# TensorE's products beside the sort handed out whole, six matmuls in a row, instead of in two parts of three

## What is computed

```
gate_feature = hidden_states * pe[i] @ gate_w + gate_b
gate_weight, gate_idx = jax.lax.top_k(gate_feature, K)          # K = 384 of 768
gate_weight = jax.nn.softmax(gate_weight, axis=-1)
gathered = jnp.take_along_axis(hidden_states, gate_idx, axis=-1)
y = y + _moe_mlp(gathered * gate_weight, eg_w[i], eu_w[i], ed_w[i])
```

## Time and profile before

| what | value |
| --- | --- |
| median of 3 runs | 6455.91 us (6451.81 to 6457.31) |
| the profiled execution: its run, its span | 6456.37 us, 6454.4 us |
| PE busy / DVE busy / ACT busy / POOL busy, of the span | 88% / 80% / 41% / 64% |
| mean granted TensorE clock | 0.969 |

### The profile page before, as it was taken

One profiled execution on the slowest core, in us unless ns is written; L12 is line 12 of the kernel. 1 busy time (PEld: TensorE's weight loads), 2 busy tenths in 40 slices (PEclk: granted clock), 3 DMA queues, 4 the chain that ended last, 5 costly groups with the idle time before them and its releaser, 6 DMA issues. The chain is left out here.

```text
span 6454.4 us, 69413 instructions
## 1 busy us (share of the span) xinstructions
PE 5694.2 (88%) x16428; PEld 2987.6 (46%) x16428; DVE 5155.9 (80%) x6434; ACT 2631.7 (41%) x4313; POOL 4120.3 (64%) x3617
## 2 busy tenths in 40 slices
PE   8989999889888888888888888888888888889888
PEld 4545555445444444444444444444444444445554
DVE  4011012999999999999999999999999999999831
ACT  0000000445454545454545454545454545544431
POOL 0543024667777777777777777777777776768630
PEclk9999999999999999999999999999999999999999
DMA  3366245000000000000000000000000000001101
GB/s 124 111 154 163 109 122 156 23 22 15 15 15 16 15 16 15 18 14 30 1 30 1 30 2 29 15 16 15 16 16 15 16 15 16 15 30 37 37 24 45
DMA packets 113766, 254.55 MB, mean 39 GB/s; under 512 B 36104, under 2 KB 46862, under 8 KB 113322
## 3 DMA queue, kind: packets, MB, share of 16 engines
q1 hardware_dynamic: 70442, 180.18, 8.0%
q0 software_dynamic: 42880, 69.46, 4.4%
HBM read 214.75 MB, written 34.58 MB: 39 GB/s over the span
## 5 line engine op out<-in xcount | busy, mean ns | idle before, releaser
L1390 PE MATMUL mask_ps<-key,neg_ident 125*125 125x480 f32 (+7 forms) x4128 | 1886.0, 578 | 477.3 <-DVE key L1787 443.3
L1485 POOL TENSOR_TENSOR pay<-pay_side,pay 125x480 int32<-125x480 int32 (+11 forms) x1075 | 1288.7, 1199 | 643.3 <-DVE pay L1810 637.3
L1669 ACT COPY mask_ps<-key 125x960 f32<-125x960 f32 (+6 forms) x1107 | 947.9, 856 | 1587.4 <-DVE pay L1827 930.6
L1477 POOL TENSOR_TENSOR pay_side<-pay 125x480 int32<-125x480 int32 (+11 forms) x1075 | 1284.6, 1196 | 355.5 <-DVE pay L1827 209.1
L1390 PEld LDWEIGHTS mask_ps<-key,neg_ident 125*125 125x125 f32 x4128 | 732.7, 193 | 1394.7 <-DVE key L1787 882.1
L1810 DVE COPY_PREDICATED pay<-mask_ps,pay 125x960 f32<-125x960 int32 (+6 forms) x1075 | 1231.8, 1146 | 74.4 <-PE mask_ps L1390 54.4
L1777 DVE TENSOR_TENSOR key<-mask_ps,key 125x960 f32<-125x960 f32 (+6 forms) x1075 | 1082.8, 1007 | 20.9 <-PE mask_ps L1390 16.9
L1787 DVE TENSOR_TENSOR key<-mask_ps,key 125x960 f32<-125x960 f32 (+6 forms) x1075 | 1083.9, 1008 | 1.1
L1390 PE MATMUL mask_ps<-key_top,neg_ident 125*125 125x480 f32 (+3 forms) x1472 | 588.3, 527 | 150.8 <-DVE key_top L1787 139.5
L1337 PE MATMUL slot_ps<-w_exp,hid 128*125 128x384 f32 x1920 | 676.1, 491 | 10.4 <-issue 8.7
L1309 PE MATMUL slot_ps<-u_feat,w_exp 128*128 128x312 f32 (+1 forms) x2304 | 666.6, 427 | 0.7 <-ACT u_feat L1564 0.7
(11 more groups left out here) (191 smaller groups left out, 5707.7 us busy)
## 6 DMA issues: line engine op xcount, KB each, us to landing
w_rel_g<-L_gnn_W SPq DMA_DIRECT2D x16, 2304.0 KB, 23.4
w_exp<-L_ffn_ed_w SPq DMA_DIRECT2D x16, 2304.0 KB, 8.4
messages_dram<-rows_g SPq DMA_DIRECT2D x12, 1875.0 KB
w_exp<-L_ffn_eg_w SPq DMA_DIRECT2D x16, 1152.0 KB, 5.4
w_exp<-L_ffn_eu_w SPq DMA_DIRECT2D x16, 1152.0 KB, 7.9
messages_dram<-rows_g SPq DMA_DIRECT2D x20, 375.0 KB
root_w_g<-L_gnn_root SPq DMA_DIRECT2D x2, 2304.0 KB
w_exp<-L_ffn_sg_w SPq DMA_DIRECT2D x4, 1152.0 KB, 5.8
```

Source lines behind the costliest of these rows:

```text
L1390: last = pe.matmul(mask, neg_ident[0:TP, 0:TP], operand, start=False, stop=True, skip_group_check=True)
L1477: pool.tensor_tensor(shares(pay_was(turn, u), turn, u)[1].bitcast(I32), first, second, ALU.add).then_inc(pays_added, 1)
L1485: pool.tensor_tensor(second, shares(pay_was(turn, u), turn, u)[1].bitcast(I32), first, ALU.subtract).then_inc(pays_taken, 1)
L1669: act.copy(seed_of(turn, u), compared(turn, u)[0]).then_inc(seeded, 1)
```

## The change

Every product is one part instead of two: `gate_parts`, `mixed_parts` and `down_parts` give the planner one weight for a product where they gave two, with the same sum, and `mixed`, `gate` and `down` write all their matmuls in one call.

```
-        gate_parts = [[4 * HALF, 3 * HALF]] * NHALF
+        gate_parts = [[7 * HALF]] * NHALF
 
         def mixed_parts(nk, nf):
-            return [[KK * TOK_HALVES[0][1]] * (nk // KK)] * (2 * nf * len(TOK_HALVES))
+            return [[nk * TOK_HALVES[0][1]]] * (2 * nf * len(TOK_HALVES))
 
         def down_parts(nf):
-            return [[KK * HALF] * (nf // KK)] * NHALF
+            return [[nf * HALF]] * NHALF
...
             def down(n, bank, t, half, nf, down_w, loads, hids, part):
-                if part == 0:
-                    if hids is not None:
-                        pe.wait_ge(hid_ready, hids + 1)
-                        pe.wait_ge(down_loaded, loads * 16)
-                    room(n)
-                for f in range(part * KK, part * KK + KK):
+                if hids is not None:
+                    pe.wait_ge(hid_ready, hids + 1)
+                    pe.wait_ge(down_loaded, loads * 16)
+                room(n)
+                for f in range(nf):
                     last = pe.matmul(slots[bank][0:TP, 0:HALF], hid[:, f, t * TP:(t + 1) * TP],
                                      down_w[:, f, half * HALF:(half + 1) * HALF], start=(f == 0), stop=(f == nf - 1))
-                if part == nf // KK - 1:
-                    last.then_inc(filled, 1)
+                last.then_inc(filled, 1)
```

More of the change, by code:

```diff
@@ L1301, in mixed @@
             def mixed(n, bank, ins, nk, weight, first, count, inputs, loads, part):
-                if part == 0:
[L1303 to L1306, removed]
-                    room(n)
-                for k in range(part * KK, part * KK + KK):
+                if inputs is not None:
+                    pe.wait_ge(emptied, inputs)
+                if loads is not None:
+                    pe.wait_ge(gu_loaded, loads * 32)
+                room(n)
+                for k in range(nk):
                     last = pe.matmul(slots[bank][:, 0:count], weight(bank, k), ins[:, k, first:first + count],
                                      start=(k == 0), stop=(k == nk - 1))
-                if part == nk // KK - 1:
-                    last.then_inc(filled, 1)
+                last.then_inc(filled, 1)
             def gate(n, bank, e, t, half, part):
@@ L1316, in gate @@
                 slot = slots[bank][0:TP, 0:HALF]
[L1317 to L1324, removed]
+                pe.wait_ge(xs_ready, e * NT + (t + 1))
+                room(n)
+                if is_set(e, t):
+                    pe.wait_ge(bias_set, (e - 1) * NEARLY + (2 * t + half + 1))
+                else:
+                    pe.matmul(slot, ones[0:1, 0:TP], gate_b[0:1, cols], start=True, stop=False)
+                for k in range(KD):
                     last = pe.matmul(slot, xs[:, t % 2, k, :], gate_w[:, k, cols], start=False, stop=(k == KD - 1),
                                      skip_group_check=is_set(e, t))
-                if part == 1:
-                    last.then_inc(filled, 1)
+                last.then_inc(filled, 1)
             def down(n, bank, t, half, nf, down_w, loads, hids, part):
-                if part == 0:
-                    if hids is not None:
-                        pe.wait_ge(hid_ready, hids + 1)
-                        pe.wait_ge(down_loaded, loads * 16)
-                    room(n)
-                for f in range(part * KK, part * KK + KK):
+                if hids is not None:
+                    pe.wait_ge(hid_ready, hids + 1)
+                    pe.wait_ge(down_loaded, loads * 16)
+                room(n)
+                for f in range(nf):
                     last = pe.matmul(slots[bank][0:TP, 0:HALF], hid[:, f, t * TP:(t + 1) * TP],
                                      down_w[:, f, half * HALF:(half + 1) * HALF], start=(f == 0), stop=(f == nf - 1))
-                if part == nf // KK - 1:
-                    last.then_inc(filled, 1)
+                last.then_inc(filled, 1)
             def gate_products(e, base, tiles=range(NT)):
```

## The result

The changed kernel takes 6729.9 us (median, 6724.13 to 6733.7) against 6453.9 us (6447.85 to 6457.31) for the kernel before beside it: a ratio of 1.043, 95% interval 1.0417 to 1.0443. It is slower by 276 us, inside the predicted range, where 198 were forecast. The profiled execution took 6727.95 us and spans 6726.1, that is 271.7 more than the earlier trace rows.

A forecast was written before the change was run, and what follows sets the result against it. VectorE was taken to set the pace in the sort, with PE close behind. Queue 118, clock 70 and ScalarE with GpSimd 10 sum to 198 us; 6454.4 + 198 + 2.0 gives 6654 us, range 6535 to 6740.

The forecast's parts named there:

- Step 1 and 2, the queue: Six matmuls in PE's queue delay the next mask past its 1.6 us cover: 7.5 us a turn, 118 us in all.
- the listed places: The 20 places of a regular turn where a product delays the next mask, worked out singly: nothing to 1.3 us each.
- step 4: The slot is filled 1.93 us later, so ScalarE's copy delays its seeds: 10 us in all, bounds 0 and 30.
- step 3: At emptied units PE's clock falls to 1.2 GHz and VectorE waits: three falls a turn, 70 us, bounds 0 and 130.
- Clock unchanged: At the emptied units PE's clock falls no more often than now: 6520 to 6600, middle 6575; chance 0.29.
- The clock falls nearly everywhere: PE's clock falls at six newly idle places in each turn, with long falls: 6734, up to 6770; chance 0.14.
- Not slower: PE's row of six keeps its clock up, masks are late only within their cover: likely 6440 to 6456; chance 0.08.

The follow-up runs named there:

- e1: The changed kernel with extra zero-matrix matmuls ahead of masks at eleven idle units of the regular turns, to hold PE's clock: 6624.1 us, ratio 1.0266.
- e10: The changed kernel with extra zero-matrix matmuls at fifteen units of a regular turn and nine of the opening: 6629.6 us, ratio 1.0273.
- e8: Against the kernel before, each product of six matmuls is cut into six parts of one, which the planner spreads: 6425.5 us, ratio 0.9959.
- e7: The kernel before with extra zero-matrix matmuls ahead of masks at its eight longest-idle units of the regular turns: 6430.3 us, ratio 0.996.

## Why the prediction was right in sign and 78 us short

**What bounds the kernel** held: VectorE's time in the sort, with PE behind it in an order that nothing can pass.

**Step 1 and 2, the queue.** Predicted 7.5 us a turn. The idle time at the listed places is 7.3 (e1), and the single places are right within 0.2 but for three: F(42) was put at 0.5 and lost 0.83, F(85) at 1.0 and lost 1.23, F(26) at 0.2 to 0.4 and lost nothing. PE takes 3.87 us for six matmuls, as worked out. What was missing is that each stall costs 0.1 us more than its idle time (last section): 15 new ones are 1.5 us a turn. In all 10.0 us with the clock held, of which 0.8 belong to step 4 and 0.5 to a fall left in e1, so 8.7: 113 us in 13 turns where 98 stood, inside the bounds of 65 to 170. Turn 15 came out as predicted (6.3), turn 1 at 8.1 instead of 4.6 and a share of step 3.

**Step 3, the clock, is the term that was mis-sized.** The mechanism was right and so was the price: a stretch of 3.4 us does 1.7 us less work, and at F(32) the fall cost 1.7. The count was wrong. I took three new falls a turn. The low clock rose by 35.8 - 17.8 = 18.0 us a turn, 5.3 stretches of 3.4 us, and 8.1 us / 5.3 = 1.5 us each. So 13 turns gave 105 us where 5 x 13 = 65 stood. Of the six places that I named (units 2, 20, 31, 34, 37, 48), the clock falls within one unit of 37 in all 13 turns, of 48 in 11, of 20 and 34 in 7, of 31 in 5, of 2 in 13 with those that start at 1. The falls at unit 5 (8 of 13) and 54 (12 of 13, 4 of 13 before) were in no list. I had looked for idle time ahead of the product only at single units. PE ahead of unit 5 in turn 8 of the kernel after:

```profile
3744.32 2.33 PE L1384 MATMUL mask_ps<-key_top,neg_ident 125*125 125x480 f32 x4 [2.35 <-DVE key_top L1781]
3746.43 5.32 PE L1332 MATMUL slot_ps<-w_exp,hid 128*125 128x384 f32 x12
```

PE idled 2.35 us ahead of the mask of unit 5, and the row of six then held it until 3751.59, 5.2 us instead of 3.9. The idle time is the child of an earlier stall: F(3) was late, VectorE late with it, and so S(5). I had counted idle time on the schedule of the kernel before, and stalls bring new idle time of PE themselves. The opening is the same error, larger: I gave it 9.4 us and next to nothing for the clock. Its first 164 us, windows of the kernel after:

```profile
1136.00:1300.00 164.00, 137.84 (x345) 70.64 (x346) 138.63 (x169) 71.97 (x111) 85.84 (x88) 0.87 0.04 16
```

The clock is 0.87 there, 0.96 before. One fall at unit 30 meets a product with its bias. PE and then VectorE of the kernel after, units 30 and 31 of the opening:

```profile
1255.52 1.64 PE L1320 MATMUL slot_ps<-gate_b,ones 1*125 1x384 f32 x2
1257.09 5.91 PE L1322 MATMUL slot_ps<-gate_w,xs 128*125 128x384 f32 x12
```

```profile
1264.79 1.24 DVE L1804 COPY_PREDICATED pay<-mask_ps,pay 125x960 f32<-125x960 int32 x1 [5.11 <-PE mask_ps L1384]
```

F(31) loses 5.11 us, the longest single wait for a mask. 24.1 us in all, 14.5 with the filling of e10. In the profiled executions 74 us are missing from the forecast: some 15 in the queue of turns 2 to 14, 47 in their clock (with the 0.5 a turn that e1 still had), the rest mostly in the opening.

**Step 4, ScalarE.** Predicted 10 us. Without the one long wait at the start, the waits for seeds went from 4.8 to 16.2 us: 11.4. Of the predicted units, 40 and 51 have them (0.49 and 0.30 in turn 8), 44 has none. L(40) in turn 8 of the kernel after:

```profile
3874.01 0.91 DVE L1771 TENSOR_TENSOR key<-mask_ps,key 125x720 f32<-125x720 f32 x1 [0.49 <-ACT mask_ps L1663]
```

The loads and GpSimd cost nothing, as predicted: VectorE waits for GpSimd 16 us in all in either kernel.

**The signs that were to show.** The row that was named, `pay` at L1810, went from 54.4 us in 85 waits to 213.7 us in 196 at L1804, where 150 or more in some 250 were foreseen; with `pay_top` and the other stages F waits 293 times instead of 92. F(21) idles 1.2 to 1.3 us in 11 of 13 turns and 2.5 to 2.7 in two, where a fall adds to it. The mean clock fell from 0.969 to 0.950. The single waits reach 2.7 us in the loop and 5.1 in the opening, where I had put at most 1.3. DVE's busy time was to stay at 5156 and is 5178.

**The rivals.** "Clock unchanged" gave 6575 for the middle; e1 with the clock nearly held is at 6624, 24 us above that rival's upper end, with the opening's clock not held. Its premise failed besides: the low clock went from 17.8 to 35.8 us a turn. "The clock falls nearly everywhere", 6734, came closest to the 6729.9 measured, and I gave it 0.14. It deserved more: its condition, a fall at nearly each of the six places, is what the trace shows at three of them and in half the turns at the others. "Not slower" needed a row of six that keeps the clock up. The clock fell instead, and with it held (e1) the row still cost 2.7%. So the advice of the Trainium skill, "TensorE: Matmul & The Clock Gate", section "HAM oscillation", to do all K tiles in one go so that the clock stays up, doesn't hold here. With all six matmuls in one go the kernel took 4.3% more time at a lower mean clock, and handed out in parts of one, at most three to a unit, 0.4% less (e8). The page's case is a loop in which TensorE waits for a DMA between K tiles; here VectorE waits for the next instruction of TensorE's queue.

## What to carry to other kernels

Where one engine works beside another in a fixed order, first measure the cover: how late may the instruction that the other engine waits for start? A block ahead of it is free up to the cover and costs its whole excess beyond, so look for the longest block that still fits (here four or five matmuls of 0.645 us), and cut finer rather than coarser when in doubt. Price the clock together with the queue: at one place the same fall cost 0.1 us with the cover unused and 1.7 with it used up, and at another, between short units, 1.2 with no product in the queue. Count the falls on the schedule as it will be with its stalls, and when cutting blocks anew, work out where the planner will put each part.

## What the runs showed of the hardware that I had not expected

**A stall costs more than its idle time.** In the earlier trace rows S(9) runs from 3623.73 for 1.17 us, to 3624.90, and F(8) starts at 3624.78: consecutive VectorE instructions overlap by 0.1 us. After a stall there is no such overlap. S(22) in the kernel after ends at 3806.57 + 1.14 = 3807.71, the idle time of 1.30 us counts from there to F(21) at 3809.02, and without the wait F(21) would have started at about 3807.6. This is where the 22 us of longer busy time come from with the same instructions: some 220 more stalls at 0.1 us. The other traces bear it out. From S(0) of the opening to S(0) of the closing VectorE runs the same 5662 instructions in all 13 kernels. Its busy time there goes from 4842.6 us with 162 stalls of over 0.15 us (e8) to 4869.0 with 425 (after), and a line through all 13 rises by 0.10 us a stall. No run was made for it alone.

**Work with zeros holds the clock.** Matmuls of a zero matrix, 420 records more, took the mean clock from 0.969 to 0.987 and the time 24 us below that of the kernel before (e7). They have to fit the cover of their own mask: at unit 49 of e10 one such mask cost 0.8 us.
